# Reordered transposes and corner copy in the attention slot, and half of the keys' stage's block transfers issued by GpSimd

## The reference

```python
mixed = silu(causal_conv(x @ W_qkv, taps of 4 tokens))
q, k, v = split(mixed)                 # 16 heads of q and k, 32 of v
q, k = l2norm(q) * DK ** -0.5, l2norm(k)
beta, g = sigmoid(x @ W_b), -exp(A_log) * softplus(x @ W_a + dt_bias)
def step(S, inp):                      # for each token
    S = S * exp(gt)
    u = (vt - k_t . S) * bt
    S = S + outer(k_t, u)
    return S, q_t . S
on = rms_norm(o) * silu(x @ W_z)       # (layer 1 gates before it normalizes)
out = on @ W_out
```

## Time and profile before

| | us |
|---|---|
| median of three runs | 4951.69 |
| lowest and highest of them | 4949.87 and 4952.98 |
| the profiled execution, its own time | 4951.72 |
| its span in the profile | 4949.9 |

### The profile page before, as it was taken

One profiled execution on the slowest core, in us unless ns is written; L12 is line 12 of the kernel. 1 busy time (PEld: TensorE's weight loads), 2 busy tenths in 40 slices (PEclk: granted clock), 3 DMA queues, 4 the chain that ended last, 5 costly groups with the idle time before them and its releaser, 6 DMA issues. The chain is left out here.

```text
span 4949.9 us, 93402 instructions
## 1 busy us (share of the span) xinstructions
PE 4443.0 (90%) x32596; PEld 3643.5 (74%) x32596; DVE 3852.1 (78%) x8126; ACT 2999.4 (61%) x9834; POOL 692.1 (14%) x740
## 2 busy tenths in 40 slices
PE   5899937999999999999969988299999999999998
PEld 3577736888888888888845877188888888887887
DVE  6838887888888888888841587788888888888886
ACT  1145526777777777777611555366666676767665
POOL 0000001122121221212200000021212122221211
PEclk8999968999999999999969999599999999999999
DMA  1035543222232222222200555322222222222222
GB/s 56 28 96 158 166 123 92 77 82 75 79 87 72 80 71 85 80 77 80 61 30 15 144 165 166 100 77 77 83 73 79 72 81 74 80 76 80 71 80 63
DMA packets 637757, 422.56 MB, mean 85 GB/s; under 512 B 458344, under 2 KB 533656, under 8 KB 636846
## 3 DMA queue, kind: packets, MB, share of 16 engines
q1 hardware_dynamic: 637294, 416.62, 29.2%
HBM read 296.24 MB, written 120.16 MB: 84 GB/s over the span
## 5 line engine op out<-in xcount | busy, mean ns | idle before, releaser
L1204 DVE SCALAR_TENSOR_TENSOR conv_l<-mix_l,taps_l,conv_l 128x512 f32<-128x512 f32 x1152 | 865.0, 751 | 270.3 <-ACT conv_l L1031 243.0
L837 PE MATMUL pj_l<-x_high,w_high_l 128*128 128x512 f32 x1280 | 588.2, 460 | 160.3 <-ACT w_high_l L1040 160.3
L837 PE MATMUL pj_l<-x_high,w_low_l 128*128 128x512 f32 x1280 | 521.1, 407 | 41.8 <-DVE W_l L1292 41.8
L837 PE MATMUL pj_l<-x_low,w_high_l 128*128 128x512 f32 x1280 | 512.5, 400 | 0.0
L1406 POOL TENSOR_TENSOR fac_l<-den_l,powers 128x4 f32<-128x4 f32 x256 | 258.0, 1008 | 1783.7 <-DVE den_l L1327 1779.8
L1005 PE MATMUL gb_l<-wo_l,gT_l 128*128 128x256 f32 x2048 | 478.7, 384 | 0.0
L1172 ACT ACTIVATE Z_l<-gb_l 128x128 f32<-128x128 f32 x1024 | 267.9, 289 | 307.1 <-PE gb_l L996 307.1
L1005 PEld LDWEIGHTS gb_l<-wo_l,gT_l 128*128 128x128 f32 x2048 | 372.6, 190 | 67.8 <-ACT Z_l L1172 24.4
L1337 DVE SCALAR_TENSOR_TENSOR x<-gb_l,fac_l,x 128x256 f32<-128x256 f32 x1024 | 413.0, 477 | 9.0
L837 PEld LDWEIGHTS pj_l<-x_high,w_high_l 128*128 128x128 f32 x1280 | 241.6, 189 | 231.3 <-ACT w_high_l L1040 160.9
L1163 ACT ACTIVATE y_l<-gb_l 128x512 f32<-128x512 f32 x256 | 153.2, 598 | 397.8 <-PE gb_l L969 393.1
(11 more groups left out here) (203 smaller groups left out, 10449.0 us busy)
## 6 DMA issues: line engine op xcount, KB each, us to landing
rows_l<-rows_dram SPq DMA_DIRECT2D x128, 1024.0 KB, 5.5
k_dram<-kT_l SPq DMA_DIRECT2D x128, 256.0 KB, 2.3
kk_dram<-key_kkS_l SPq DMA_DIRECT2D x128, 256.0 KB, 2.4
kq_l<-k_dram SPq DMA_DIRECT2D x128, 256.0 KB, 3.2
kkS_l<-kk_dram SPq DMA_DIRECT2D x128, 256.0 KB, 5.7
w_raw_l<-in_wx SPq DMA_DIRECT2D x32, 640.0 KB
own_dram<-key_kkS_l SPq DMA_DIRECT2D x1024, 16.0 KB, 1.7
lane_k_l<-own_dram SPq DMA_DIRECT2D x32, 512.0 KB, 4.4
```

The source lines that it names most:

```text
L837: ins = nc.tensor.matmul(pj_bank(c, t), wt[:, k, t, :], xt[:, k, :, at], start=(k == 0 and n == 0), stop=(k == KD - 1 and n == 2))
L1204: ins = nc.vector.scalar_tensor_tensor(out, mix[:, t, :, i:i + P], wt(i), out, ALU.mult, ALU.add)
```

## The change

In the keys' stage the blocks of the first value head of each slot are still stored by SyncE, and those of the second by GpSimd, which gets a program of its own: 64 slots of four transfers, each set behind the copy of its products. The buffer of products has three parts instead of two. The waits for stores count both senders. To make room for the third buffer, VectorE's work array `step` is laid into the array of decays, which adds a wait: the scan of a group starts only behind the solve of the group before.

In the attention slot, three steps change their place. TensorE does the keys' transposes behind the products with Xd, not ahead of them, and the queries' transposes ahead of its waits for X and Z, not behind them. ScalarE copies X's last corner ahead of the queries' squares where c > 0; in a head's first chunk the order stays.

```diff
-    STORES = 1 + QUADS * GROUPS
+    STORES = 1 + QUADS
+    RINGK = 3
...
-        kkS = sb("key_kkS", [P, 2, WIDE])
+        kkS = sb("key_kkS", [P, RINGK, WIDE])
...
-        step = sb("lane_step", [P, MOST, (QUAD // 2) * (QUAD // 2 - 1)])
+        step = decay[:, :, :, :].rearrange("p h i j -> p h (i j)")
...
                 def store_products(q):
                     h, c = divmod(q, CHUNKS)
                     sp.wait_ge(kk_cp, q + 1)
-                    sp.dma_start(m.kk_dram[L][h, c], kkS[:, q % 2, :]).then_inc(kk_out[q % 2], 16)
+                    sp.dma_start(m.kk_dram[L][h, c], kkS[:, q % RINGK, :]).then_inc(kk_out[q % RINGK], 16)
                     for r in range(QUADS):
                         rows = slice(r * QUAD, (r + 1) * QUAD)
-                        own = by4(kkS[rows, q % 2, :])[:, :, rows]
-                        for g in range(GROUPS):
-                            lane = r * QUAD + (c * GROUPS + g) * BATCH
-                            sp.dma_start(m.own_dram[L][h, lane:lane + BATCH].rearrange("b i j -> i b j"),
-                                         own).then_inc(kk_out[q % 2], 16)
+                        own = by4(kkS[rows, q % RINGK, :])[:, :, rows]
+                        lane = r * QUAD + c * GROUPS * BATCH
+                        sp.dma_start(m.own_dram[L][h, lane:lane + BATCH].rearrange("b i j -> i b j"),
+                                     own).then_inc(kk_out[q % RINGK], 16)
 
                 def load_lanes(h):
-                    for par in range(2):
-                        sp.wait_ge(kk_out[par], 16 * STORES * (h + 1) * CHUNKS // 2)
+                    for i in range(RINGK):
+                        sp.wait_ge(kk_out[i], 16 * STORES * len(range(i, (h + 1) * CHUNKS, RINGK)))
+                        sp.wait_ge(own_out[i], 16 * QUADS * len(range(i, (h + 1) * CHUNKS, RINGK)))
...
                 def copy_products(q):
                     act.wait_ge(kk_mm, q + 1)
-                    if q >= 2:
-                        act.wait_ge(kk_out[q % 2], 16 * STORES * (q // 2))
-                    nc.scalar.activation(kkS[:, q % 2, :], kk[:, q % 2, :], ACT.Copy).then_inc(kk_cp, 1)
+                    if q >= RINGK:
+                        act.wait_ge(kk_out[q % RINGK], 16 * STORES * (q // RINGK))
+                        act.wait_ge(own_out[q % RINGK], 16 * QUADS * (q // RINGK))
+                    nc.scalar.activation(kkS[:, q % RINGK, :], kk[:, q % 2, :], ACT.Copy).then_inc(kk_cp, 1)
...
                     dve.wait_ge(gains_ok, last_of[k] + 1)
+                    if k >= 1:
+                        dve.wait_ge(solve, STEPS * k)
...
+            @block.gpsimd
+            def _(pool):
+                for q in range(SLOTS):
+                    h, c = divmod(q, CHUNKS)
+                    pool.wait_ge(kk_cp, q + 1)
+                    for r in range(QUADS):
+                        rows = slice(r * QUAD, (r + 1) * QUAD)
+                        lane = r * QUAD + (c * GROUPS + 1) * BATCH
+                        pool.dma_start(m.own_dram[L][h, lane:lane + BATCH].rearrange("b i j -> i b j"),
+                                       by4(kkS[rows, q % RINGK, :])[:, :, rows]).then_inc(own_out[q % RINGK], 16)
...
                     pe.wait_ge(z32_cp, it + 1)
-                    if not last:
-                        keys_token_major(nh, ncn, False)
                     if not first:
...
                     ins.then_inc(dx_mm, 1)
                     if not last:
+                        keys_token_major(nh, ncn, False)
                         project(nh, ncn, 2, 0, False)
...
                     fill(3)
+                    if not last:
+                        queries_token_major(nh, ncn, False)
                     pe.wait_ge(x_in, 32 * (it + 1))
                     pe.wait_ge(x_cp, 4 * it + 1)
                     for g in range(GROUPS):
                         pe.wait_ge(z_cp[g], it + 1)
-                    if not last:
-                        queries_token_major(nh, ncn, False)
...
                     if not last:
                         silu_z(nh, ncn, 0)
+                    if c > 0:
+                        copy_corner(it)
+                    if not last:
                         square_queries(nh, ncn)
-                    copy_corner(it)
+                    if c == 0:
+                        copy_corner(it)
```

More of the change, by code:

```diff
@@ L328, in key_blocks @@
             "gains_ok", "lane_cleared", "prep", "solve", "tt_ok", "minus_ok"))
-        k_out, kk_out, t_out, tt_out = by_parity("k_out"), by_parity("kk_out"), by_parity("t_out"), sem("tt_out")
+        k_out, t_out, tt_out = by_parity("k_out"), by_parity("t_out"), sem("tt_out")
+        kk_out = [sem(f"kk_out_{i}") for i in range(RINGK)]
+        own_out = [sem(f"own_out_{i}") for i in range(RINGK)]
         bank = lambda b: slice(b * P, (b + 1) * P)
```

## The result

The changed kernel took 4971.19 us (median of 6 runs, 4968.67 to 4976.27) against 4951.78 us for the kernel before on the same chip (6 runs, 4949.87 to 4956.1). The ratio is 1.004 with a 95% interval of 1.0027 to 1.0052: slower by 0.4%, 19 us, where 30 had been forecast. The profiled execution has a span of 4967.0 us.

The account below looks back on a forecast made before the run. TensorE, with nearly no holes, bounds the attention; the keys' stage has holes from ScalarE's waits for stores. 4951.7 + 72 (attention) - 42 (keys' stage) = 4982 us, range 4937 to 5110.

Parts of the forecast that it names:

- Keys' transposes behind the Xd products: Attention, every slot: ScalarE from its copy L1068 on and VectorE's second convolution 0.61 us later; earlier products gain nothing.
- Queries' transposes ahead of the wait: Attention slot: transposes fill TensorE's hole before ScalarE's Z copies end, so L939 starts 0.15 us earlier, not 0.56.
- Corner copy: Attention, c > 0: squares end 0.61 + some 0.5 us later, L1309 starts 0.70 us late, 0.8 in the third chunk.
- short overlap: Attention: ScalarE's corner copy of 0.78 us was to delay the queries' squares some 0.5 us, the pipes overlapping shortly.
- The clearance: Attention: VectorE's slack at L1224; with L1309's 0.29 us wait it was to take 0.4 us off the lateness.
- Where it meets TensorE: Attention: VectorE's lateness reaches TensorE, 29 us in layer 0 and 43 in layer 1, +72 in all, bounds 45 and 85.
- Keys' stage: SyncE's relief and third buffer shorten stalls (18 us) and lift the clock (5): -21 a layer, -42, bounds -15, -65.
- GpSimd's issue: Keys' stage: 1.0 us a transfer, range 0.5 to 2.0, four hidden beneath a 5.4 us slot; cover ends at 1.35.
- (a): Rival: GpSimd bounds the keys' stage from 1.35 us an issue; 5130 us at 1.7; chance 0.24 together with (d).
- (b): Rival: in the attention the lateness of ScalarE's copy is absorbed, TensorE keeps its lead, 4883 us; chance 0.12.
- (c): Rival: both parts small, attention at its lower bound or below, keys at their best, 4935 to 4960 us; chance 0.09.
- (d): Rival: VectorE's solve holds GpSimd's issues up in the keys' stage, slot 6 us, 5024 us; chance 0.24 together with (a).

Follow-up runs that it names:

- move_keys: The kernel before with only the keys' transposes moved behind the Xd products: 5042.06 us, ratio 1.0185.
- ring3_sync: The kernel before with three buffers in the keys' stage, SyncE still sending all blocks, attention as before: 4952.75 us, ratio 0.9996.
- pool_ring2: The kernel before with GpSimd sending half of the blocks, but two buffers, attention as before: 4882.15 us, ratio 0.9854.
- keys_only: The kernel before with the whole changed keys' stage (three buffers, GpSimd's half), attention as before: 4875.15 us, ratio 0.9847.
- pool_all: The kernel before with three buffers and GpSimd sending all eight blocks of a slot, attention as before: 4878.18 us, ratio 0.9839.
- that reordering of ScalarE, one line: Against the changed keys' stage with only the queries' transposes moved (4861.92 us): ScalarE's second-projection copies ahead of the keys' squares; 4830.58 us.

## Why the prediction was right or wrong

The sign, the order of the two parts and the total (4982 against 4971, inside the range) were right, the total in part by luck: both terms were too small, by some 22 and 33 us, both lay outside their own bounds (85 and -65), and the errors partly cancelled. By its own steps:

- **Keys' transposes behind the Xd products: mechanism right, size short.** The copy came 0.76 us later, not 0.61. The forecast took the products' time alone. The transposes also take longer in the new place, 0.66 us instead of 0.60 (the rows of L866 and L849). And the Xd products start later behind the projection than the transposes did in that place, 1.06 us into the slot against 0.97. 0.61 + 0.06 + 0.09 are the 0.76. Why either is so was not tried. That the earlier Xd products gain nothing held: the wait of TensorE for W is the same 0.4 us in 62 slots, 20.7 us before and 24.0 after.
- **Queries' transposes ahead of the wait: right.** L955 came 0.03 us earlier in that slot, where 0.15 had been forecast; the difference is about the 0.15 that the first step was short. What the step didn't say is that this edit alone gains 14 us, and that without it the keys' move would put its 0.7 us into every slot of both layers (`move_keys`).
- **Corner copy: place right, two terms wrong.** The "short overlap" was not there: the squares start 1.53 us late, 0.76 + 0.77, against a forecast of 1.1. The clearance was short too. Before, L1224 did not wait for the squares, as the forecast had it; they ended at 2160.47, 0.31 us ahead of it, and it followed VectorE's own convolution. That clearance took 0.29 off (L1244 is 1.24 late), and L1309's wait took 0.24 (from L1224 to L1309 there were 1.65 us before and 1.41 after): 0.53 in all, not 0.4. So 1.53 - 0.53 = 1.00 us, where 1.1 - 0.4 = 0.70 was forecast: the lateness was 0.43 short and the slack 0.13.
- **Where it meets TensorE: right.** Layer 0: +0.31, +0.19, +0.97, +0.98 us against +0.2, +0.2, +0.8, +0.7; layer 1: +0.73, +0.94, +1.05, +0.99 against +0.61, +0.70, +0.80, +0.70. The slack in the first chunk of layer 0 (0.4 us) and its absence in the third and fourth was read rightly from the earlier trace rows. The second chunk's 0.2 was called a guess and came true by luck: the slack there is larger, 0.94 us of lateness in layer 1 against 0.19 in layer 0. The sum, 94 us, lies above the bound of 85: that bound moved only the slack of one chunk and left 0.61 and the clearance fixed, though each slot of 128 rests on them.
- **Keys' stage: cause half right, two terms short.** The stalls of TensorE for ScalarE's burst fell from 25.6 to 6.0 us (longest 1.4, forecast 1.3), 19.6 us for a forecast 18. But TensorE's idle time fell by 29.8: L450's wait for ScalarE (5.4 us, once) and L440's (0.8) went too, and 4.1 us at the stage's end, where the last copy stood for a block's store. The clock gave 11.9 us and not 5: it went to 1.00 for the whole stage, while I had let some of the falls stand. The stretch behind the last copy gives 3 to 4 us back (41.7 and 41.1 us gained up to the last copy, 38.4 and 36.9 in all), against 2 forecast for the lanes' load; what part of it is that load is not shown. The third buffer, which the forecast named beside SyncE's relief, is worth nothing alone (`ring3_sync`) and little beside GpSimd's half (`pool_ring2` -73.0 us, `keys_only` -75.0, with intervals that overlap). VectorE's new wait, costed at nothing, is in `ring3_sync` together with that buffer; it was not tried by itself. The gain, -75 us, lies outside the bound of -65.
- **GpSimd's issue:** 0.55 us, not 1.0, near the lower end of 0.5 to 2.0. SyncE's row was the nearer neighbour, not GpSimd's small arithmetic; nothing ahead of the result could tell which. The price didn't matter, as the cover ends at 1.35.
- **The rivals.** (a) is refuted: even all eight issues fit, with 0.57 us each in `pool_all`. (b) is refuted, since the lateness was not absorbed. (c) would have needed the attention to be small. (d), VectorE holding GpSimd up, is refuted as a price of every slot: VectorE is busy 275.35 of 340 us in the stage, and the issues take 551 ns at the median. But its mechanism is there, for the one instruction of each group that has a single input. GpSimd and VectorE in the changed kernel:

```profile
374.56 3.47 POOL L637 DMA_DIRECT2D own_dram<-key_kkS_l  x3 [3.20 <-ACT key_kkS_l L509]
```
```profile
374.50 2.32 DVE L614 TENSOR_SCALAR lane_t_l<-lane_k_l 128x2048 f32<-128x2048 f32 x1
```

Of 512 issues ten take over 1 us (1.1 to 2.6), and each of them overlaps L614 and ends 0.1 us behind it; the 352 that meet only two-input products and subtractions take 551 ns at the median and 737 at most. The rule of the Trainium skill (SBUF — State Buffer, "Who interferes with whom") that a two-input tensor_tensor doesn't lock descriptor writing out agrees with these rows. That the one-input L614 ran in the 2-port mode of that rule no row shows: it takes 2.3 us for 2048 elements, as long as the two-input L609. It costs nothing here, since a slot has 3.2 us of GpSimd's idle time.

## What to carry to other kernels

When two edits ride in one change, measure each alone: here a loss of 94 us hid a gain of 75, and the halves added up, while the edits inside one slot did not. Before moving an operation behind another, count what is queued behind its consumer on the next engine, and look for idle time there that other ready work could fill: that reordering of ScalarE, one line, was worth 31 us. Judge such an edit against the kernel that lacks only it, or it is given gains of its neighbours. When an engine waits for a store, ask first how full the queue is that issues it, and what stands behind the stores in it; here a deeper buffer only moved the wait.

## What was new about the hardware

- GpSimd issued these block transfers (16 KB, short runs) at 0.55 us each in steady state, four in 2.18 us, close to SyncE's 0.48 us. They landed 2.3 us from issue at the median, and SyncE's half in the same kernel 2.2; SyncE's alone had 1.7 before. So both became slower side by side, and GpSimd's are hardly slower than SyncE's.
- Ten issues of GpSimd that stood at the start of VectorE's one-input L614, or came during it, lasted until it ended (up to 2.6 us); four that had begun 0.35 us or more ahead of it took their 0.55 us, as those under two-input operations do at the median.
- SyncE's eight issues took 3.81 us in the earlier trace rows but 6.43 us in the stretch of `ring3_sync` shown above: the price of one isn't fixed. What sets it stays open.
- TensorE's granted clock in layer 0's keys' stage was 1.00 (the 2.4 GHz level) with 6.1 us of idle time in 340, where it had been 0.95 with 35.9 us of 381.7; the same matmuls took 11.9 us less of busy time.
- The same four transposes took 0.60 us before and 0.66 us behind the 64x64 products. Why was not tried.
